# Pair 1's maximum pass cut into six units between the steps of pair 0's second front

## The reference

```python
# first attention ("s = 0" in the kernel)
attn = jnp.einsum('bihd,bjhd->bhij', q, k) * scale[None, :, None, None]
attn = jnp.where(mask[None, None], -jnp.inf, attn)     # all but the first token: not itself
attn = softmax(attn, axis=-1)
# second attention ("s = 1")
logits = jnp.einsum('bqhd,bkhd->bhqk', Q, K) * hd ** (-0.5)
logits = (logits - mean) / (std + 1e-5)                # over the keys
probs = softmax(gamma * logits, axis=-1)
# experts
h = relu(einsum('btd,edf->ebtf', x, W1) + b1);  y = einsum('ebtf,efd->ebtd', h, W2) + b2
```

## Time and profile before

| | |
|---|---|
| median of 3 runs | 1238.06 us (1237.32 to 1239.3) |
| the profiled execution | 1242.59 us, of which the span from the first to the last instruction is 1240.8 us |
| mean granted clock of PE | 0.94 of full speed |
| PE busy | 1114.1 us (90%) |
| DVE busy | 680.4 us (55%) |
| ACT busy | 397.6 us (32%) |
| the first round | from 247.85 us of the span on, where pair 0's tokens are turned in |

### The profile page before, as it was taken

One profiled execution on the slowest core, in us unless ns is written; L12 is line 12 of the kernel. 1 busy time (PEld: TensorE's weight loads), 2 busy tenths in 40 slices (PEclk: granted clock), 3 DMA queues, 4 the chain that ended last, 5 costly groups with the idle time before them and its releaser, 6 DMA issues.

```text
span 1240.8 us, 19314 instructions
## 1 busy us (share of the span) xinstructions
PE 1114.1 (90%) x7726; PEld 816.6 (66%) x7726; DVE 680.4 (55%) x1874; ACT 397.6 (32%) x905; POOL 55.6 (4%) x90
## 2 busy tenths in 40 slices
PE   7898887898889999999999999999999989888895
PEld 4343354554577678667866785688578757676795
DVE  3357777454555566556646564665557653643432
ACT  1223221322323343324243334334343333232321
POOL 6001110000000000000000000000000000000000
PEclk9898897999989899989998999899999998898998
DMA  9000034412042104310530152024203320040000
GB/s 307 1 1 0 1 125 82 88 43 46 8 86 66 29 5 106 63 18 10 111 63 9 28 111 45 9 49 90 45 9 73 66 45 2 1 88 8 1 10 9
DMA packets 38481, 60.79 MB, mean 49 GB/s; under 512 B 5060, under 2 KB 30264, under 8 KB 37944
## 3 DMA queue, kind: packets, MB, share of 16 engines
q1 hardware_dynamic: 36112, 56.84, 21.4%
q10 hardware_dynamic: 2280, 2.72, 0.8%
HBM read 42.76 MB, written 16.34 MB: 48 GB/s over the span
## 4 chain that ended last, share of the span: by engine, by line
PE 62%; DVE 15%; ACT 4%; DMA 3%; issue 2%; SPq 1%; POOL 0%; DVEq 0%; ACTq 0%; POOLq 0%
PE PS L677 15%; PE PS L655 12%; DVE mx L1349 7%; PE PS L776 6%; PE PS L870 5%; PE PS L811 5%; PE PS L784 5%; PE PS L817 3%; PE PS L879 2%; PE PS L826 2%; DMA qst<-mrows 1%; PE PS L908 1%; PE PS L999 1%; DVE acc L705 1%; ACT probs L1087 1%
## 5 line engine op out<-in xcount | busy, mean ns | idle before, releaser
L677 PE MATMUL PS<-w,hid 128*128 128x192 f32 x1152 | 233.1, 340 | 2.6 <-DVE acc L705 1.9
L690 ACT ACTIVATE hid<-PS,b 128x370 f32<-128x370 f32 x192 | 109.3, 569 | 321.7 <-PE PS L655 320.1
L677 PEld LDWEIGHTS PS<-w,hid 128*128 128x128 f32 x1152 | 199.1, 198 | 13.5 <-issue 4.8
L1349 DVE TENSOR_REDUCE mx<-PS 128x2 f32<-128x356 f32 x288 | 128.8, 521 | 130.8 <-PE PS L811 100.6
L1087 ACT ACTIVATE probs<-PS 128x356 f32<-128x356 f32 x288 | 110.8, 484 | 21.9 <-PE PS L811 12.4
L655 PE MATMUL PS<-x2T_hi,w_hi 128*128 128x370 f32 x192 | 91.2, 475 | 0.0
L811 PE MATMUL PS<-kst,qst 96*128 96x178 bf16 x384 | 66.6, 269 | 12.8 <-DMA kst<-scr_k 5.5
L826 PE MATMUL PS<-masks,ident_bf 128*128 128x256 bf16 (+1 forms) x288 | 75.4, 262 | 0.0
L870 PE MATMUL PS<-probs,va 128*17 128x178 f32 x1536 | 67.3, 315 | 6.4 <-ACT probs L1087 6.4
L776 PE MATMUL PS<-xT,w_at 96*96 96x370 f32 x192 | 67.1, 493 | 2.9 <-ACT xT L1047 2.0
L655 PE MATMUL PS<-x2T_lo,w_hi 128*128 128x370 f32 x192 | 66.0, 344 | 0.0
(11 more groups left out here) (228 smaller groups left out, 1760.9 us busy)
## 6 DMA issues: line engine op xcount, KB each, us to landing
qst<-scr_q SPq DMA_DIRECT2D x96, 144.0 KB, 4.8
scr_q<-qs SPq DMA_DIRECT2D x16, 432.0 KB, 3.3
scr_k<-ks SPq DMA_DIRECT2D x16, 432.0 KB, 3.3
kst<-scr_k SPq DMA_DIRECT2D x16, 432.0 KB, 5.0
kst<-scr_k SPq DMA_DIRECT2D x16, 288.0 KB, 5.9
cols<-in_x_cols SPq DMA_DIRECT2D x6, 392.0 KB, 10.0
w<-in_w SPq DMA_DIRECT2D x1, 2304.0 KB, 26.2
kst<-scr_k SPq DMA_DIRECT2D x16, 144.0 KB, 6.3
```

The source lines that it names most:

```text
L677: ins = nc.tensor.matmul(tile_psum((6, 7), i), hid[u % 2][:, 128 * i:128 * i + 128], w2[:, u, :], start=(j == 0 and i != 1), stop=(j == FT ...
L690: nc.scalar.activation(hid[u % 2][:, 0:XN], PS[:, 4 + u % 2, 0:XN], ACT.Relu, bias=b1[:, u:u + 1]).then_inc(S["h_ready"], 1)
L1349: nc.vector.tensor_reduce(out, PS[:, g, 0:T2].rearrange("p (b j) -> p b j", b=2), AX.X, ALU.max)\
```

## The change

In the first round only (m is None), pair 1's maximum pass is no longer a block of its own behind pair 0's second front. Its six units are issued one by one between the steps of that front: unit 0 behind the transposed tokens, unit 1 behind the query, unit 2 behind the key, unit 3 behind the transposed keys, unit 4 behind the Gram matrices, unit 5 behind their product with the query. They use banks 4 to 6, so that they don't meet the front's banks 0 to 3. The waits for the stacked queries and keys of pair 1 and for its values move to the place ahead of unit 0. On DVE the reductions move likewise: nine of them (units 0 to 2) ahead of the split of the keys, three ahead of the masked Gram, three behind it, three behind the product. Most of the unread matmuls between the front's steps are taken out: 50 in all before, 10 after. Nothing else is added or removed; the arithmetic is the same. Later rounds are as before. The core of the diff:

```diff
 WARM = {
-    "norm": 4, "query": 9, "key": 6, "value": 0, "kc": 4, "g": 3, "u": 5, "ss": 4,
-    ("max", 0): (0, 0, 0, 0, 0, 0), ("split", 0): 15, ("rows", 0): 22, ("exp", 0): (0, 0, 0, 0, 0, 0), ("out", 0): 0,
+    "norm": 0, "query": 2, "key": 0, "value": 0, "kc": 0, "g": 0, "u": 0, "ss": 4,
+    ("max", 0): (0, 0, 0, 0, 0, 0), ("split", 0): 4, ("rows", 0): 22, ("exp", 0): (0, 0, 0, 0, 0, 0), ("out", 0): 0,
...
+        def pe_max_unit(pe, s, r, u, first=0):
+
+            pe_logits(pe, s, r, u, SROWS, qst[s], kst[s], S["s_used", s], S["s_psum", s], first)
...
+                def unit(u):
+                    if beside:
+                        pe_max_unit(pe, 0, a, u, 4)
+
                 pe_turn_in(pe, 1, b)
+                if beside:
+                    pe_stacked(pe, 0, a)
+                    pe.wait_ge(S["v_ready", 0], at(a, 1, 1))
+                unit(0)
                 moe.point("norm")
                 pe_query(pe, 1, b)
+                unit(1)
                 moe.point("query")
                 pe_key(pe, 1, b)
+                unit(2)
...
-                pe_max_pass(pe, 0, a, moe)
+                if m is not None:
+                    pe_max_pass(pe, 0, a, moe)
...
+        def dve_max_unit(dve, s, r, u, first=0):
+            for g in range(3):
+                dve.wait_ge(S["s_psum", s], at(r, 3 * HH, 3 * u + g + 1))
+                out = mx[:, 0:2, 2 * u + g] if g < 2 else mx[:, 2, 2 * u:2 * u + 2]
+                nc.vector.tensor_reduce(out, PS[:, first + g, 0:T2].rearrange("p (b j) -> p b j", b=2), AX.X, ALU.max)\
+                    .then_inc(S["s_used", s], 1)
```

More of the change, by code:

```diff
@@ L800, in pe_value, with pe_logits @@
             pe_tokens(front(s, r), 4 * s + 2, xT[s], S["v_psum", s])
-        def pe_logits(pe, s, r, u, rows_, still, move, read, filled):
+        def pe_logits(pe, s, r, u, rows_, still, move, read, filled, first=0):
             for bank in range(3):
@@ L810, in pe_logits @@
                     for b in range(2):
-                        ins = nc.tensor.matmul(PS[:, bank, T * b:T * b + T], still[0:rows_, h, TP * b:TP * b + NTXT],
+                        ins = nc.tensor.matmul(PS[:, first + bank, T * b:T * b + T], still[0:rows_, h, TP * b:TP * b + NTXT],
                                                move[0:rows_, h, TP * b:TP * b + T], start=(b == 0), stop=(s == 1),
@@ L816, in pe_logits @@
                         for b in range(2):
-                            ins = nc.tensor.matmul(PS[64 * b:64 * b + 64, 2, T * g:T * g + T],
+                            ins = nc.tensor.matmul(PS[64 * b:64 * b + 64, first + 2, T * g:T * g + T],
                                                    still[0:rows_, 2 * u + g, TP * b + NTXT:TP * b + TP],
@@ L822, in pe_logits @@
                 if s == 0:
-                    own = PS[:, bank, 0:T2].rearrange("p (b j) -> p b j", b=2)
+                    own = PS[:, first + bank, 0:T2].rearrange("p (b j) -> p b j", b=2)
                     own, m = (own[:, :, 0:NTXT], masks[:, 0:2 * NTXT]) if bank < 2 else (own[:, :, NTXT:T], masks[:, 2 * NTXT:T2])
@@ L889, in pe_out, with pe_deviation @@
             pe_tokens((2, 3), 4 * s + 3, oT, S["pr_psum", s])
-        def pe_deviation(pe, b, moe):
+        def pe_deviation(pe, b, moe, unit):
             for h in range(2):
@@ L899, in pe_deviation @@
             ins.then_inc(S["kc_psum"], 1)
+            unit(3)
             moe.point("kc")
@@ L909, in pe_deviation @@
             ins.then_inc(S["g_psum"], 1)
+            unit(4)
             moe.point("g")
@@ L916, in pe_deviation @@
             ins.then_inc(S["u_psum"], 1)
+            unit(5)
             moe.point("u")
@@ L932, in pe_round @@
                     pe.wait_ge(S["gate_used"], at(b, 1, 0))
+                beside = m is None
+                def unit(u):
+                    if beside:
+                        pe_max_unit(pe, 0, a, u, 4)
                 pe_turn_in(pe, 1, b)
+                if beside:
+                    pe_stacked(pe, 0, a)
+                    pe.wait_ge(S["v_ready", 0], at(a, 1, 1))
+                unit(0)
                 moe.point("norm")
                 pe_query(pe, 1, b)
+                unit(1)
                 moe.point("query")
                 pe_key(pe, 1, b)
+                unit(2)
                 moe.point("key")
@@ L942, in pe_round @@
                     pe.wait_ge(S["v_ready", 0], at(a, 1, 1))
-                pe_deviation(pe, b, moe)
+                pe_deviation(pe, b, moe, unit)
                 moe.point("ss")
@@ L1293, in dve_norm1, with dve_front1 @@
             return scaled
-        def dve_front1(dve, r, a, moe, last):
+        def dve_front1(dve, r, a, moe, last, units):
             ch = chain(dve, "dve_front1", r)
@@ L1308, in dve_front1 @@
             last.finish()
+            for u in units[0:3]:
+                dve_max_unit(dve, 0, a, u, 4)
             moe.point("norm")
@@ L1318, in dve_front1 @@
             moe.point("kc")
+            for u in units[3:4]:
+                dve_max_unit(dve, 0, a, u, 4)
             dve.wait_ge(S["g_psum"], at(r, 1, 1))
@@ L1324, in dve_front1 @@
             ins.then_inc(S["g_ready"], 1)
+            for u in units[4:5]:
+                dve_max_unit(dve, 0, a, u, 4)
             moe.point("g")
@@ L1330, in dve_front1 @@
                                     q32[1][:, :, :, 0:T], ALU.mult).then_inc(S["prod_ready"], 1)
+            for u in units[5:6]:
+                dve_max_unit(dve, 0, a, u, 4)
             moe.point("u")
@@ L1342, in dve_front1, with dve_max_split @@
             return query
+        def dve_max_unit(dve, s, r, u, first=0):
[4 more added lines that the diff above has]
+                    .then_inc(S["s_used", s], 1)
         def dve_max_pass(dve, s, r, moe):
             for u in range(HH):
[L1346 to L1350, removed]
+                dve_max_unit(dve, s, r, u)
                 moe.point(("max", s), u)
+            dve_max_split(dve, s, r)
+        def dve_max_split(dve, s, r):
             ch = chain(dve, f"dve_max{s}", r)
@@ L1418, in dve_round @@
             if b is not None:
-                query = dve_front1(dve, b, a, moe, last)
+                query = dve_front1(dve, b, a, moe, last, tuple(range(HH)) if m is None else ())
                 if a is None:
@@ L1425, in dve_round @@
             if a is not None:
-                dve_max_pass(dve, 0, a, moe)
+                if m is None:
+                    dve_max_split(dve, 0, a)
+                else:
+                    dve_max_pass(dve, 0, a, moe)
                 moe.point(("split", 0))
```

6 lines of the change are left out of this document (4 added, 2 removed).

## The result

The changed kernel takes 1228.69 us (median of 13 runs, 1224.57 to 1235.83) against 1239.17 for the kernel before beside it on the same chip (13 runs, 1232.28 to 1246.52). The ratio is 0.9923 [0.9899, 0.9947], by which it takes 9.5 us less (6.6 to 12.5). Both were run a second time: the changed kernel 0.9945 [0.991, 0.998], the kernel before against itself 1.0013 [0.999, 1.0035]. So the changed kernel is faster, by more than the forecast 5.8 and with the median under the range. The profiled execution took 1231.46, with a span of 1229.4; that of before 1240.8.

The account below looks back on a forecast made before the run. Bound: the first round's chain of waits, with 7.94 us of DVE reductions. Query loads 6.3 earlier, less 0.5 for half clock, give 5.8 off the median 1238.06: 1232.2 us, range 1229.6 to 1235.2.

Parts of the forecast that it names:

- The 18 reductions leave the place behind the front: First round: pair 1's DVE reductions, 7.94 us, go into the front's waits; the rows of maxima start 7.06 earlier.
- signs of being wrong: First round: ACT's steps ending after 275, a row copy over 2.04, or a clock under 1.00 between 249 and 273.
- The front's lengthening, 1.55: First round's front: the units inserted there make ACT's four deviation steps end 1.55 us late; bounds 0.53 to 6.4.
- Six units of 1.06, 6.4 us, take their place, and the clock there was 1.00: First round's front: the units replace 29 unread matmuls of at most 6.1 us on PE.
- slower: Rival: without unread matmuls the front falls to half clock from the query on, 11.5 longer; 1243.8 us; chance 0.04.
- The clock in the exponential pass: First round: after a PE stop of 1.8, 3.5 us at half clock cost 1.2, of which 0.7 is hidden.
- The 0.5 that was to be left of it: Exponential pass, first round: net half-clock cost of 0.5 us after the wait for the stacked queries; bounds 0 to 1.7.
- They now come 6.30 earlier: Pair 0's stacked queries land at 289.51, moved with DVE's scaled query; its maximum pass starts 6.3 earlier.
- Everything behind (...) hangs on this chain, so 6.3 stays to the end: Output, second exponential pass and later rounds: the first round's 6.3 us gain is handed on in full.
- theory P: Follow-up runs' theory: rounds 2 and 3 answer by where round 1's end stands against clock changes, jumping beyond the shift.

Follow-up runs that it names:

- e4: Changed kernel with six more unread matmuls behind unit 3 and ten more ahead of the exponential pass, first round; 1227.69 us, ratio 0.991 [0.9882, 0.9938].
- e6: Changed kernel with only six more unread matmuls behind unit 3 in the first round; 1229.88 us, ratio 0.9934 [0.9901, 0.9966].
- e5: Changed kernel with rounds 2 to 8 left out and the added unread matmuls of e4; 408.34 us (406.88 to 409.29).
- e8: e4 plus two unread matmuls behind each of five units of the second attention's maximum pass, rounds 2 to 7, and a moved wait; 1242.47 us, ratio 1.0012.
- e12: The kernel before once more, nothing edited, timed against itself; 1240.77 us, ratio 1.0013 [0.999, 1.0035].
- e3: Kernel before with 40 more unread matmuls in round 1, between pair 1's maximum pass and the transposed maxima; 1237.72 us, ratio 0.9988 [0.9965, 1.0011].
- e11: The changed kernel once more, nothing edited; 1231.31 us, ratio 0.9945 [0.991, 0.998].
- e9: e6 with eight more unread matmuls ahead of the second rows of maxima in round 1; 1234.13 us, ratio 0.9947 [0.9916, 0.9977].
- e10: e6 with 14 more unread matmuls ahead of the second rows of maxima in round 1; 1229.98 us, ratio 0.9928 [0.9897, 0.9959].

## Why the prediction was right and wrong

- **"The 18 reductions leave the place behind the front"**, and ACT's deviation steps end last: right. ACT goes from the last rem step to mrows without a stop. Of the prediction's signs of being wrong one came, a clock under 1.00 between 249 and 273; ACT's steps ended at 274.92, just under 275.
- **The front's lengthening, 1.55**: mis-sized. With the clock held (e4, e6) it is 1.0, and the rows of maxima come 7.7 earlier (267.46 - 243.54 = 23.92 behind xT against 31.65) where 7.06 was forecast, the second ones 6.1 to 6.8 earlier against 6.3.
- **"Six units of 1.06, 6.4 us, take their place, and the clock there was 1.00"**: this step failed. The sum over the front was about right (PE was busy for 12.74 of 14.00 us up to the stop, and for 20.27 of 23.00 in the front before), but the forecast took one clock for the whole front and did not go through its stops one by one. Behind unit 3, where PE waits for DVE's values, a stop of 0.95 was followed by 10.2 us at half clock. That was the mechanism of the rival "slower", at a part of its price: 3.1 us in place of 11.5, because the fall came behind the Gram matrices, not from the query on. The forecast had a stop of 1.0 that passed at clock 1.00, and the kernel before passed one of 0.82 at this very place; one stop that passed was no evidence for another.
- **The clock in the exponential pass**: right in kind, with 3.4 us at half clock against 3.5 forecast, and in what it adds to the pass, 1.3 against 1.2. The 0.5 that was to be left of it can't be told from nothing: the wait for the query load covers it, and e6 with the fall has its second rows of maxima 0.3 behind e4 but 0.3 to 0.4 ahead of e5 and e8 without it. The rule cited with it, that the check on PE's activity runs free (the Trainium skill, "TensorE: Matmul & The Clock Gate", Part 1), would let one stop fall on either side from one execution to the next. For the stops in the front and ahead of the exponential pass no trace here shows that: they fell alike in each trace of one kernel, though xT lay at 247.77 and at 243.74. Later the traces agree with it: in round 1 of the kernel before, e12 is at half clock from 320.5 for 3.4 us where the first trace is at 1.00, and rounds 2 and 3 differ in the two traces of each kernel.
- **"They now come 6.30 earlier"**, the query loads: mis-sized, because the forecast moved the load with DVE's scaled query, us for us. In the changed kernel the scaled query came 3.7 earlier and the load 2.8, with the front's clock kept 6.9 and 6.0 to 6.7: the store ahead of the loads took 4.1 to 4.9 in place of 3.3.
- **"Everything behind (...) hangs on this chain, so 6.3 stays to the end"**: this step failed, and with it the sum. e3 put 6.2 into round 1 and lost nothing measurable; the same instructions of rounds 2 and 3 took 240.3 to 249.9 in nine traces, with the granted clock. Three traces with 15.7 to 15.9 us at half clock in them took 240.3 to 240.4 (the changed kernel, e6, e3), four with 25.3 to 25.7 took 246.1 to 246.4 (the kernel before, e11, e9, e10), one with 18.8 took 243.6 (e4), and one with 35.1 249.9 (e12). In these traces a shift was handed on only where the clock behind it was granted alike (e6 against the changed kernel: 3.4 at round 1's gl, 4.0 at the end, both from xT).

That the time moved the way that was forecast, and further, is in part luck: the first round gave less than its share, and more came from where the sum had nothing. In both pairs of traces 4.0 to 4.5 of the gap are of round 1: 2.9 to 3.0 up to the second rows of maxima, and 1.1 to 1.5 from there to gl. The rest lies in later rounds, with the granted clock: 5.6 and 3.4 in rounds 2 and 3, and 1.3 and 2.6 from gl of round 3 to gl of round 8. From xT to the end both pairs differ by 10.4, but two traces of one kernel differ by 6.8. That a timed gap over 4 us is due to the change at all is likely, since it came in both comparisons (6.6 to 12.5 us, then 2.5 to 11.2, which has 4 in it), but how much of it belongs to the executions that were drawn can't be told. What decides which pattern a round takes stays open: it is the same kernel in two executions, so not the order of instructions alone, and the time at which round 1 ends doesn't sort them (343.43 long, 344.62 short, 346.84 the longest, 347.29 short).

One thing does sort the nine traces: how far ahead of round 1's gl the last fall to half clock began. Where it began 1.2 and 1.4 us ahead (the changed kernel, e6), rounds 2 and 3 took 240.3 to 240.4; at 1.7 (e11, e9) they took 246.4, at 2.5 (e12) 249.9. Where it began further ahead, 4.6 (e3) goes with 240.4, 5.1 (e4) with 243.6, and 5.2 and 5.5 (e10, the kernel before) with 246.1 to 246.3. No run set this distance on purpose, so it is a lead and not a cause that is shown. By it the place of the round's end against the changes of the clock counts, as theory P had it, and a shift of half a us could move the time by 6.

No version tried beats the changed kernel beyond what can be told: e4 and e6 have their second rows of maxima 3.5 to 3.9 earlier, but their times aren't told apart from its time.

## What to carry to other kernels

Where a change fills an engine's waits with real work and takes the unread matmuls out, look at each wait by itself: the sum over the stretch was kept here, and half clock behind one stop of 0.95 us took back 3.1 of the 7.7 us won up to the rows of maxima. Put a price on half clock by who paces the stretch: in a pass paced by DVE it cost nothing, and taking it away there raised the mean clock and not the speed. Look at what comes along with such matmuls: a wait that was moved for their bank cost 0.7 us a round. And before a saving early in a kernel is added to the end, delay that place by about as much: if the time stays, the later rounds vary by themselves, and the saving must be read from its own round in several traces.

## What was not expected of the hardware

- A delay of 6.2 us in round 1 changed the time by a ratio of 0.9988 [0.9965, 1.0011].
- The same 1754 matmuls took from 240.26 to 249.85 us, at mean granted clocks of 0.97 to 0.93.
- The falls to half clock in the front and the exponential pass of round 1 were the same in each trace of a kernel; those further back, and of rounds 2 and 3, were not.
- A maximum pass took 7.93 us at a mean granted clock of 0.77 and 7.92 at 1.00.
- The same store of 432 KB took 3.3 to 3.4 us in one order of the round and 4.1 to 4.9 in the other.
